# A graph kernel's setup: table parts, code sums and digits move to GpSimd, rows are scaled in three lots

## The reference, cut to what matters

```python
def gnn_layer(x, W, b, src, dst):                 # twice, relu between
    msg = x[src] @ W.T + b
    return segment_sum(msg, dst) / maximum(count(dst), 1)

h = maximum(layernorm(x), 0)
x = x + gnn_layer(relu(gnn_layer(h, W1, b1)), W2, b2)
h = maximum(layernorm(x), 0)
m = relu(concat(h[src], emb[edge_type]) @ msg_W.T + msg_b)
agg = segment_sum(m, dst) / maximum(count(dst), 1)
z = h + agg @ upd_W.T + upd_b
x = x + layernorm(z) * ln_g + ln_b
```

## Time and profile before

| what | value |
|---|---|
| median of 3 runs | 1577.69 us (1574.48 to 1584.54) |
| the profiled execution's own time | 1576.79 us |
| its span | 1574.8 us |
| busy in the span | PE 1325.9, DVE 1203.7, ACT 1203.6, POOL 1077.3 us |
| first unit's one-hots begin on VectorE | 59.97 us |
| first gather begins on GpSimd | 52.19 us |
| last one-hots of layer 0 | about 605 us |

### The profile page before, as it was taken

The page is one execution under the profiler, slowest core; times in us unless marked ns, Lnnn a source line. Parts: engine busy times, 40 slices in busy tenths (PEclk is TensorE's granted clock), DMA queues, the critical chain, the costliest instruction groups (busy, mean ns, idle before and its releaser), DMA issues.

```text
span 1574.8 us, 34937 instructions
## 1 busy us (share of the span) xinstructions
PE 1325.9 (84%) x13033; PEld 1221.4 (78%) x13033; DVE 1203.7 (76%) x2525; ACT 1203.6 (76%) x1381; POOL 1077.3 (68%) x1015
## 2 busy tenths in 40 slices
PE   0488889888888989499999899589998999999993
PEld 0388778877887888377777777489998999998993
DVE  7799999999999997123444433478898998998895
ACT  6578888887898897767888888466776777767773
POOL 1457767777676662877777777277777777777771
PEclk9899999999999999899999999789999999999996
DMA  6222322222232233575656556556665666665651
GB/s 174 77 84 84 94 83 87 88 88 89 82 95 91 90 102 114 162 202 137 183 156 184 157 170 178 172 158 170 184 183 160 191 189 170 178 181 170 178 165 54
DMA packets 174119, 218.72 MB, mean 139 GB/s; under 512 B 27496, under 2 KB 147976, under 8 KB 173944
## 3 DMA queue, kind: packets, MB, share of 16 engines
q1 hardware_dynamic: 146296, 159.74, 32.8%
q0 software_dynamic: 27648, 56.68, 14.3%
HBM read 165.43 MB, written 50.88 MB: 137 GB/s over the span
## 4 chain that ended last, share of the span: by engine, by line
DVE 31%; PE 22%; POOL 18%; issue 15%; ACT 8%; DVEq 4%; DMA 3%; SPq 0%; POOLq 0%; ACTq 0%
PE banks L1343 21%; POOL rows_all L981 17%; DVE region_b L1818 5%; DVE dst_hot L1818 3%; ACT near_wide L1285 2%; DVE src_hot L1818 2%; DMA rows_all<-table,src_all 2%; DVE src_in_all L1818 2%; DVE hot L1818 2%; DVE region_b L1850 1%; ACT hslot L1046 1%; DVEq L1910 1%; DVEq L2358 1%; DVE region_b L1843 1%; DVE digit_hot L1818 1%
## 5 line engine op out<-in xcount | busy, mean ns | idle before, releaser
L981 POOL DMA_INDIRECT rows_all<-table,src_all x864 | 1025.0, 1186 | 422.5 <-issue 266.7
L1265 ACT ACTIVATE near<-banks 128x1024 fp32r<-128x1024 f32 (+2 forms) x288 | 237.4, 856 | 86.1 <-PE banks L1343 83.7
L1285 ACT ACTIVATE near_wide<-near_in 128x1024 fp32r<-128x1024 uint8 (+1 forms) x288 | 238.7, 886 | 66.9 <-PE banks L1343 66.5
L1343 PE MATMUL banks<-near,htab 128*128 128x256 f32 x1764 | 282.6, 300 | 0.0
L1343 PE MATMUL banks<-near_wide,htab 128*128 128x512 f32 x882 | 231.7, 413 | 10.5 <-ACT near_wide L1285 10.3
L1343 PEld LDWEIGHTS banks<-near,htab 128*128 128x128 f32 x1764 | 234.4, 196 | 3.7
L1270 ACT ACTIVATE near_bytes<-near 128x1792 uint8<-128x1792 f32 (+1 forms) x144 | 229.2, 1591 | 4.6
L1343 PE MATMUL banks<-hot,rows_all 128*128 128x128 f32 x1728 | 221.3, 283 | 11.4 <-DMA rows_all<-table,src_all 11.4
L1343 PEld LDWEIGHTS banks<-hot,rows_all 128*128 128x128 f32 x1728 | 214.0, 200 | 14.7 <-issue 13.0
L1307 ACT ACTIVATE dst_wide<-dst_slots 128x1792 fp32r<-128x1792 bf16 (+1 forms) x120 | 190.0, 1584 | 30.6 <-PE banks L1343 17.3
L1343 PEld LDWEIGHTS banks<-near_wide,htab 128*128 128x128 f32 x882 | 163.1, 194 | 57.1 <-ACT near_wide L1285 25.7
(11 more groups left out here) (236 smaller groups left out, 2009.3 us busy)
## 6 DMA issues: line engine op xcount, KB each, us to landing
near_in<-near_tab SPq DMA_DIRECT2D x108, 192.0 KB, 2.7
near_tab<-near_bytes SPq DMA_DIRECT2D x72, 224.0 KB
rows_all<-table,src_all POOLq DMA_INDIRECT x864
near_tab<-near_bytes SPq DMA_DIRECT2D x72, 192.0 KB
src_in_all<-src_tab SPq DMA_DIRECT2D x60, 224.0 KB
region_b<-type_tab SPq DMA_DIRECT2D x60, 224.0 KB
src_in_all<-src_tab SPq DMA_DIRECT2D x60, 192.0 KB
region_b<-type_tab SPq DMA_DIRECT2D x60, 192.0 KB
```

What stands on the lines that cost most here:

```text
L981: nc.gpsimd.indirect_dma_start(out=to[:, c, :], out_offset=None, in_=tab[layer], in_offset=bass.IndirectOffsetOnAxis(ap=cols[:, c:c + 1], ...
L1265: nc.scalar.activation(near[slot][:, at:at + own, :], near_ps[h][:, 0:own, :], ACT.Copy)\
L1285: nc.scalar.activation(wide_piece(n, h), near_slot(n)[:, :, at:at + size, :].rearrange("p b j f -> p j b f"), ACT.Copy).then_inc(near_wide ...
L1343: return nc.tensor.matmul(to, left, right, start=start, stop=stop)
```

## The change

The second parts of the table (`rests`) leave VectorE for GpSimd, all 14 halves. So do the sum of position and type (the shift by 7 becomes a product with 128) with its cast into `codes`, and the digits, of which VectorE keeps the two shifts by 4 (now right after `edge_tiles`, signalled with `edges_split`); the low digit is now made as destination minus 16 times the high part. `dst_high` moves to the space of `hot1`, `dst_low` falls away. Every one of GpSimd's eleven instructions on codes and digits waits for the one before it (`pool_step`). Then come the 14 halves, each when ScalarE has made it, then the memset of `count2`, and only then GpSimd's gathers.

Rows are scaled in three lots (steps 0 and 1, 2 and 3, 4 to 6). VectorE's setup is written in a new order: the first block's sort is one piece behind the edge codes, with no `rests` between and no wait for ScalarE's rows, and `sort_same(1)` stands before `sort_first(2)`. `sort_codes(0)` waits for the third of GpSimd's steps, the first group's one-hot for all second parts, the second group's for the digits.

```diff
--- before.py
+++ after.py
@@ -248,8 +248,8 @@
-        dst_high = placed("dst_high", [P, GROUPS, C], i32, "x_or_cnt", 2 * NEAR + NEAR // 4)
-        dst_low = placed("dst_low", [P, GROUPS, C], i32, "x_or_cnt", COUNT_SPACE + 1664)
+        dst_high = placed("dst_high", [P, GROUPS, C], i32, "hot1", 0)
+        assert GROUPS <= P
@@ -457,8 +459,9 @@
         NV = len(UNITS_POST)
         CONSTS = 13
         CLEARED = 4
-        SOONER = 4
-        ROW_PARTS = (slice(0, SOONER * STEP), slice(SOONER * STEP, TILES))
+        ROW_LOTS = (0, 2, 4)
+        ROW_PARTS = (slice(0, 2 * STEP), slice(2 * STEP, 4 * STEP), slice(4 * STEP, TILES))
+        CODE_STEPS = 3
         MARGIN = 40
         APART = 7
         FB_ALL = GROUPS * WINDOWS
@@ -490,6 +493,19 @@
             def wait(self):
                 self.eng.wait_ge(dve_step, self.base + self.n)
+
+        class Count_steps:
+
+
+            def __init__(self, eng):
+                self.eng, self.n = eng, 0
+
+            def chained(self, *instructions):
+
+                for make in instructions:
+                    make().then_inc(pool_step, 1)
+                    self.n += 1
+                    self.eng.wait_ge(pool_step, self.n)
         class Count:
@@ -987,6 +1003,34 @@
                     last = nc.gpsimd.memset(limits[:, k, own], float(value))
             last.then_inc(cleared, 1)
+            pool_steps = Count_steps(pool)
+            types_i = far[:, 0:BLOCK_COLS].bitcast(i32)
+            low_src, type_place = (rows[0][:, :, :].rearrange("p c f -> p (c f)").bitcast(i32)[:, k * BLOCK_COLS:(k + 1) * BLOCK_COLS]
+                                   for k in range(2))
+            by_step = lambda a: a[:, FIRST_GROUP:NB[0] * GROUPS_STEP].rearrange("p (n g) -> p n g", g=GROUPS_STEP)
+            by_chunk = lambda a: a[:, :].unsqueeze(2).broadcast_to([P, GROUPS, C])
+            pool.wait_ge(edges_split, 1)
+            pool_steps.chained(
+                lambda: nc.gpsimd.tensor_single_scalar(type_place, types_i, float(P), op=ALU.mult),
+                lambda: nc.gpsimd.tensor_tensor(type_place, type_place, low_src, ALU.add),
+                lambda: nc.gpsimd.tensor_copy(codes[:, 0, :], type_place),
+                lambda: nc.gpsimd.tensor_copy(block_high[:, :], base_high[:, :]),
+                lambda: nc.gpsimd.tensor_copy(by_step(block_high), by_step(base_high)[:, :, 0:1]
+                                              .broadcast_to([P, NB[0] - B, GROUPS_STEP])),
+                lambda: nc.gpsimd.tensor_tensor(dst_high[:, :, :], dst_high[:, :, :], by_chunk(block_high), ALU.subtract),
+                lambda: nc.gpsimd.tensor_copy(digits[:, :, 1, :], dst_high[:, :, :]),
+                lambda: nc.gpsimd.tensor_tensor(dst_high[:, :, :], dst_high[:, :, :], by_chunk(block_high), ALU.add),
+                lambda: nc.gpsimd.tensor_single_scalar(dst_high[:, :, :], dst_high[:, :, :], -float(DIGIT), op=ALU.mult),
+                lambda: nc.gpsimd.tensor_tensor(dst_high[:, :, :], dst_high[:, :, :],
+                                                dst_all[:, :].rearrange("p (g c) -> p g c", c=C), ALU.add),
+                lambda: nc.gpsimd.tensor_copy(digits[:, :, 0, :], dst_high[:, :, :]))
+            for i in range(STEPS):
+                for h in range(2):
+                    pool.wait_ge(h_ready[h], 2 * i + 2)
+                    nc.gpsimd.tensor_tensor(htab2[:, tiles(i, h), 1, :], hslot[i % ROW_SLOTS][h],
+                                            htab2[:, tiles(i, h), 0, :].bitcast(fp32), ALU.subtract).then_inc(rest_h[h], 1)
+            nc.gpsimd.memset(count2[:, :], 0.0).then_inc(digits_ready, 1)
+
             def add_rows(z, v):
                 n = len(tiles_of(v))
                 return nc.gpsimd.tensor_tensor(z[:, 0:n, :], z[:, 0:n, :], xres[:, in_unit(v), :], ALU.add)
@@ -1231,10 +1275,10 @@
             make_std(0)
             for i in range(STEPS):
-                if i == 2:
-                    make_std(1)
-                if i in (0, SOONER):
-                    act.wait_ge(norm_ready, 1 if i == 0 else 2)
+                if i + 1 in ROW_LOTS[1:]:
+                    make_std(ROW_LOTS.index(i + 1))
+                if i in ROW_LOTS:
+                    act.wait_ge(norm_ready, ROW_LOTS.index(i) + 1)
                 own = hslot[i % ROW_SLOTS]
                 if i >= ROW_SLOTS:
                     act.wait_ge(rows_stored[i % ROW_SLOTS], 32 * (i // ROW_SLOTS))
@@ -1740,13 +1784,6 @@
-            def rests(i, layer, value):
-
-                for h in range(2):
-                    dve.wait_ge(h_ready[h], i * 2 + (layer * 2 * STEPS + 2))
-                    V.tensor_tensor(htab2[:, tiles(i, h), 1, :], value[h], htab2[:, tiles(i, h), 0, :].bitcast(fp32), ALU.subtract)\
-                        .then_inc(rest_h[h], 1)
-
@@ -1775,17 +1811,15 @@
                 dve.wait_ge(edges_in, EDGE_LOADS)
                 chained(lambda: V.tensor_single_scalar(int_a, block_src, 7, op=ALU.arith_shift_right))
                 V.tensor_copy(tile_flat[:, :], int_a).then_inc(edges_used, 1)
+                dve.wait_ge(edges_used, 1)
+                V.tensor_single_scalar(int_a, block_src, P - 1, op=ALU.bitwise_and)
+                V.tensor_single_scalar(base_high[:, :], base_all[:, :], 4, op=ALU.arith_shift_right)
+                V.tensor_single_scalar(dst_high[:, :, :].rearrange("p g c -> p (g c)"), dst_all[:, :], 4,
+                                       op=ALU.arith_shift_right).then_inc(edges_split, 1)
             def edge_codes(k):
-                if k == 0:
-                    dve.wait_ge(edges_used, 1)
-                    chained(lambda: V.tensor_single_scalar(int_a, block_src, P - 1, op=ALU.bitwise_and))
-                    chained(lambda: V.tensor_single_scalar(int_b, types_i, 7, op=ALU.logical_shift_left))
-                elif k == 1:
-                    chained(lambda: V.tensor_tensor(int_a, int_a, int_b, ALU.add),
-                            lambda: V.tensor_copy(codes[:, 0, :], int_a))
-                elif k == 2:
+                if k == 2:
                     chained(lambda: V.tensor_tensor(per_group(rel), per_group(dst_all),
                                                     base_all[:, :].unsqueeze(2).broadcast_to([P, GROUPS, C]), ALU.subtract))
                 elif k == 3:
@@ -1851,28 +1885,6 @@
                 steps.wait()
                 chained(lambda: V.tensor_reduce(out=rank1[:, b * BC:(b + 1) * BC], in_=earlier[:, :, 0:14], axis=AX.X, op=ALU.add))
-            def make_digits(k):
-
-                if k == 0:
-                    for h in range(2):
...
-                steps.wait()
-                V.tensor_copy(digits[:, :, 0, :], dst_low[:, :, :])
-                V.tensor_tensor(digits[:, :, 1, :], dst_high[:, :, :], block_high[:, :].unsqueeze(2).broadcast_to([P, GROUPS, C]),
-                                ALU.subtract).then_inc(digits_ready, 1)
-
             def digit_runs(b):
@@ -1919,6 +1931,8 @@
+                    if b == 0:
+                        dve.wait_ge(pool_step, CODE_STEPS)
@@ -2004,47 +2018,38 @@
             row_stats(0)
             row_stats(1)
+            mean_and_var(0)
             dve.wait_ge(rows_laid, 1)
             sort_tiles(0)
-            edge_codes(0)
+            make_norm(0)
             row_stats(2)
-            edge_codes(1)
             row_stats(3)
-            mean_and_var(0)
+            mean_and_var(1)
             edge_codes(2)
-            make_norm(0)
+            make_norm(1)
             row_stats(4)
+            row_stats(5)
+            row_stats(6)
+            mean_and_var(2)
             edge_codes(3)
-            row_stats(5)
             edge_codes(4)
-            row_stats(6)
-            mean_and_var(1)
             edge_codes(5)
+            make_norm(2)
             edge_codes(6)
-
-            own = None
             sort_first(1)
-            for i in range(STEPS + 1):
-                if i == 2:
-                    make_norm(1)
-                if i < STEPS:
-                    rests(i, 0, hslot[i % ROW_SLOTS])
-                if i < 2:
-                    sort_same(0, i)
-                elif i == 2:
-                    sort_own()
-                elif i == 3:
-                    sort_ranks(0)
-                elif i == 4:
-                    own = sort_codes(0, 0)
+            sort_same(0, 0)
+            sort_same(0, 1)
+            sort_own()
+            sort_ranks(0)
+            own = sort_codes(0, 0)
             sort_codes(0, 1, own)
             sort_hot()
             sort_tiles(1)
+            sort_same(1, 0)
+            sort_same(1, 1)
             sort_first(2)
             sort_slots(0, 1)
             make_hots(0)
-            sort_same(1, 0)
-            sort_same(1, 1)
             def make_hot(s, cols, counts=False):
                 to = hot_b[s] if counts else hot[s][:, :, :]
@@ -2435,6 +2440,10 @@
                             dve.wait_ge(summed[ring], done)
                         if this.n == 0:
```

(7 more changed lines are left out.)

18 lines of the change are left out of this document (3 added, 15 removed).

## The result

| | time before | time after | ratio, 95% interval |
|---|---|---|---|
| first measurement | 1579.85 us (11 runs, 1574.48 to 1584.54) | **1570.76 us** (11 runs, 1567.87 to 1577.95) | 0.9955 [0.9939, 0.9972] |
| the same kernel again | 1577.56 us (29 runs) | 1573.97 us (12 runs, 1569.34 to 1576.97) | 0.9977 [0.9959, 0.9995] |

The change makes the kernel faster by 1 to 10 us (the ends of the two intervals), some 5 us by the mean of the two ratios. Forecast was 4 us slower. The time lies in the range (1562 to 1590) and within 1%, but the sign was wrong: the expected loss didn't come. All runs count, but for one of the kernel before, which took 6765.10 us in its slow state and stays out of the ratios.

What follows compares the result with a forecast made beforehand. VectorE was taken to bound layer 0, with layers 1 and 2 following in series. −15.0 us of work plus 19.0 us of stall gave +4.0 us on 1576.8, so 1581 us; range 1562 to 1590.

Steps and rivals of the forecast that it cites:

- VectorE bounds layer 0, and a microsecond in the setup reaches its end: Layer 0, to about 590 us, runs at VectorE's pace; a microsecond added or removed in its setup queue reaches program end.
- 15.0 us leave VectorE's queue: VectorE's queue: second parts, codes, digits and sort_same(1) leave, less added shifts and third lot: 15.0 us less.
- 29.0 us of reads come to GpSimd: GpSimd in the setup, from near 12 us: codes, digits and 14 second parts, 29.0 us of instructions that read SBUF.
- The stall of 19.0 us: VectorE in the setup: GpSimd's 29.0 us of reads hold it up, less 10 covered; ends 16.3 and 29.0 us.
- One-input copies, casts and compares: VectorE in the setup: perhaps not held by GpSimd's reads, some 2.5 us; if held, the sum 2 us later.
- The new waits: ScalarE's step 3 waits for step 0's second part; rows end near 55 us, gathers start near 60; costed at nothing.
- The first one-hots: End of VectorE's setup: make_hots(0) starts some 7 us later than 59.97 us.
- Rival 1: VectorE beside GpSimd in the setup: engines overlap freely, no stall, 1561.8 us; chance 0.17.
- rival 2: VectorE beside GpSimd in the setup: only 16-bit instructions are free, some 9 us of stall go, 1572 us; chance 0.17.
- Rival 3: GpSimd's integer instructions on codes and digits take twice 12.5 us, all blocking: +16.5 us, 1593 us; chance 0.09.
- Rival 4: First block: VectorE's 3.4 us gain from the digits isn't passed on, ScalarE and PE being nearly as busy: 1584 us; chance 0.07.

Runs made afterwards that it cites:

- the sums: Kernel before with 16 GpSimd additions of 512 fp32 columns in a spare corner added to the setup, nothing else changed: 1583.34 us, ratio 1.0032.

## Why the prediction was wrong

- **VectorE bounds layer 0, and a microsecond in the setup reaches its end**: right. Counted from VectorE's start, 2.7 us put in gave 2.8 at the third reduction, and 7.7 taken out with the reads gave 7.7 (9.8 against 2.1). At the end of layer 0 it is 1.7 and 7.5, or 8.7 against the second profile of after.
- **15.0 us leave VectorE's queue**: right. 2.1 us of lead at the third reduction and 13.0 of stall are 15.1 (1.6 and 12.5 in the second profile: 14.1); with the second parts only written it is 15.1.
- **29.0 us of reads come to GpSimd**: the sum was right, 29.1 us without its own waits, but with two errors that cancel. The integer products take 1.67 and 2.29 us where I had 0.71 and 1.03 (+2.2 us); the 832-column sums take 1.63, 1.63 and 1.96 instead of 2.06, and the second parts and casts a little less.
- **The stall of 19.0 us**: this step failed. It was mis-sized: 13.0 measured, below my own lower end of 16.3. I wrote that each GpSimd instruction costs VectorE its whole length unless VectorE is in something that doesn't ask, and gave 10 us for that. The cover was right (10.0 us). What failed is "its whole length": of the 19.1 us left, VectorE lost only 13.0. The other 6 us are three things. A stretched instruction's own length passes inside the wait (2.6 us). Where VectorE got in first, GpSimd waited, and VectorE lost nothing, and two-input instructions ran freely beside the end of the integer product (22.11 and 22.79): both are in the 4.2 us beside instructions of normal length, less GpSimd's waits of 1.8. And 1.2 us lie beside an idle VectorE. −15.0 + 13.0 = −2.0, which is the lead at the third reduction (2.1). My rows had one such hint: at 633.22 GpSimd's own instruction took 1.63 us for 1.09, which is a wait that VectorE doesn't pay. I read it as evidence of the stall and still charged all of it to VectorE.
- **One-input copies, casts and compares**: undecided in the forecast, now shown. A copy took 1.19 us for 0.24 and a tensor-scalar 0.90 for 0.17 in after, a cast 1.18 for 0.46 beside the sums. They are held, some of them even beside memsets (0.50 for 0.18). The Trainium skill (SBUF — State Buffer, "Who interferes with whom") says so of the two-port modes; the trace agrees. By that rule alone the stall would have been larger than mine, and it was smaller.
- **The new waits**: ScalarE's third lot waited 2.55 us for VectorE's variances (33.57), not for second parts as I wrote. The gathers start at 53.6, not near 60, and ScalarE's rows end at 51.8, not 55. All hidden by the 13.2 us of idle time before its first `near`, as costed.
- **The first one-hots**: 62.14 and 61.80 against a forecast of some 67; the stall's error of 6.0 us covers the difference.
- **Rival 1** (free overlap) and **rival 2** (16-bit instructions free): refuted. The f16 sum at 42.76 is held for 1.08 us, and without the second parts' reads the one-hots come 8.4 us earlier. Rival 2's time (1572) is near the result only because the stall is smaller everywhere, not for its reason. **Rival 3** (integer instructions double): true of the two products alone (2.4 and 2.2 times the forecast), and per us they hold the least. **Rival 4** (digits' gain not passed on): refuted, the lead goes from 0.8 us behind to 2.2 ahead across that place, and with the digits back there it hardly moves (3.5 to 3.6).

**What stays open.** The lead of 2.8 to 3.9 us at the end of layer 0 is less than the first ratio gives (7.1 us) and about the second's (3.6). Of this lead 0.9 to 1.7 us came only behind the third reduction, and no run shows why. The profiled after gained another 4.6 us in layers 1 and 2, at a granted clock of 0.967 against 0.953; its second profile, at 0.958, lost its lead there: its span, 1575.1 us, is no shorter than that of before. No run shows the change to be the cause of the clock, and I don't count that part to it.

## What to carry to other kernels

Moving elementwise work from VectorE to an idle GpSimd isn't free when VectorE is the bound: price the stall, here 13.0 us for 29.1 us of reads (0.45 per us; 0.39 in a bare test with sums), and compare it with what the work costs VectorE. Reads cost VectorE nothing beside statistics, reductions or its waits, and memsets little (1.1 us for 28 of them). Before moving, try the order alone: it gave nearly as much here as order and move together, and with part of the move, and the digits in VectorE's own wait, it had the largest lead. The ratio belongs to this mix of instructions.

## What the runs showed of the hardware that I had not expected

- An int32 product by a number on GpSimd takes 2.29 us for 832 columns and 1.49 for 512 (2.75 to 2.9 ns a column), where an int32 to bf16 cast takes 0.88 and 0.62 and a sum of two operands 1.96. The slow one holds VectorE's instructions the least: 0.18 us per us, against 0.22 of the casts and 0.39 of the float sums.
- A sum whose second operand is broadcast along the columns takes 1.63 us for 832 columns, one with two full operands 1.96; a sum of a tile with itself takes 1.04 us for 512, against 1.27 for two different operands.
- GpSimd memsets leave VectorE's two-input instructions at their normal length (0.19 us at 42.22), but not all one-input ones (0.50 for 0.18 at 41.69, 0.55 for 0.24 at 33.51).
